# A new static order of instructions on every engine of a chunked linear-attention kernel

## The chip, the core and the metric

The kernel runs on one core of a Trainium2 chip. The metric is the device time of one execution in microseconds (us); lower is better. The time before is 1025.33 us, the median of 3 runs (1024.25 to 1025.99).

## What is computed

The reference takes x of shape (2, 4096, 512) and, per token, does this:

```
outer(h)  = LN(h + routed_attention(h)) * ln_g + ln_b
x1 = x  + 0.5 * outer(LN(x))
x2 = x1 + linear_attention(LN(x1))          # 16 heads of width 32, causal
y  = x2 + 0.5 * outer(LN(x2))

linear_attention(x):
  q, k, v = x @ Wq.T, x @ Wk.T, x @ Wv.T
  pq, pk  = elu(q) + 1, elu(k) + 1
  S_t = S_(t-1) + pk_t (outer) v_t ;  z_t = z_(t-1) + pk_t
  out_t = (pq_t S_t) / (pq_t . z_t + eps) ;  result = out @ Wo.T + bo
```

Both kernels leave out the routed attention inside the two outer blocks and compute LN(LN(h)) * ln_g + ln_b there; the linear attention is computed whole. The recurrence over t is done in chunks of 128 tokens.

## The kernel before, in words

**Tiles.** A chunk is 128 tokens of each of the two batch rows (b = 0, 1); there are 32 chunks. Matrices are split into a high and a low half in f16 and each product is made of three passes (`PASSES`), so one projection of one batch row is 12 matmuls of 128x512 (`project`, L1122). Per chunk and batch row TensorE does: `project_k`, `project_q`, `project_v` (from XT, the transposed normalised x), four groups of `scores` (KS times QS, into the two banks SC), two halves of `attend` (the chunk's own part and the carried state SS, into AV), two halves of `update` (the state's increment, also into AV), and `project_out` (from AT, the transposed attention output).

**Stages.** The body of one step handles several chunks. For a step whose `now` is chunk s, the scores and the attention belong to s, the projections of q, k, v to s+1, the loading and first normalisation (`front_*`) to s+2, the final normalisation and the store (`back_*`, `store_y`) to s-1. The step's `prev` is the same with all chunks one lower, so a body ends the previous chunk and starts the next. `run` unrolls the first five and the last six bodies and loops over the rest, two bodies a turn. As the end of one body is followed by the start of the next, an operation that is moved from `prev` at the top to `now` at the bottom has not moved at all; only the cyclic order matters.

**Engines.** Each engine has a block of its own with a list of operations and a hand-written order (`body`: SyncE L345, GpSimd L499, ScalarE L691, VectorE L1020, TensorE L1230). Nothing but semaphores ties the engines: an operation first waits for its producers and for the readers of the buffer that it overwrites, and everything behind it in its engine's order waits too. XT, QN, ATTN, AT and the two banks PJ have a single buffer per batch row.

**SyncE** issues every transfer, in this order per chunk: `next_x` (L286, load of 512 KB of x), `store_y` (L341, store of 512 KB), `turn_x(0)`, `turn_x(1)` (L296, DMA transposes XH to XT), `turn_k(1)`, then for the next chunk's tiles `turn_k(0)` (L309, KN to KS), `turn_q(0)` (L322, QN to QS), `turn_attn(0)` (L333, ATTN to AT), `turn_q(1)`, `turn_attn(1)`. `turn_x(b)` must wait until `project_v(b)` has read the old XT.

**TensorE**'s order per chunk: k(0), k(1), scores(1,0), scores(1,1), q(0), scores(1,2), scores(1,3), attend(0), q(1), update(0), v(0), attend(1), v(1), then scores(0,0) of the next chunk, update(1,0), update(1,1), scores(0,1), out(0), scores(0,2), scores(0,3), out(1). The first `project_k(0)` of the next chunk waits for `x_turned[0]`.

**The chain from the attention to the next x.** After `attend(1)`: `sums(1)` (ScalarE L671), `reciprocals(1)` (VectorE L938), `quotient(1)` (L949), `attn_half(1)` (ScalarE L679), `attn_low(1)` (VectorE L968), then SyncE: `turn_attn(1)`, `next_x`, `store_y`, `turn_x(0)`.

**Hand-offs of the bank PJ[0].** `project_k(0)` fills it, `exp_relu_k(0)` (ScalarE L602, L603) and `phi_k(0)` (VectorE L914) read it, then `project_q(0)` may start. `exp_relu_q(0)` (L611), `phi_q(0)` (L900), `q_half(0)` (L620) and `low_q(0)` (VectorE L907) follow, then `project_v(0)` may start. After it `low_v(0)`, then `project_out(0)`, read by `add_out(0)` (VectorE L979). `x1_bias` (GpSimd L415) needs `add_out(1)`, and `front_x1(0)` (VectorE L853) needs `x1_bias`.

Of the kernel before, what the change touches and what calls it, by code (L numbers as in the profile page):

```python
# [12 lines left out]
GROUPS = E // P  # L13
# [51 lines left out]
def build(nc, x, Wq, Wk, Wv, Wo, attn_bo, ln_g, ln_b, out):  # L65
    with ExitStack() as ctx:
# [196 lines left out]
        def _(sp):  # L263
# [80 lines left out]

            def body(st):  # L345
                now, prev = ops(st), ops(st.before())
                prev.turn_k(0)
                prev.turn_q(0)
                prev.turn_attn(0)
                prev.turn_q(1)  # L350
                prev.turn_attn(1)
                prev.next_x()
                prev.store_y()
                prev.turn_x(0)
                prev.turn_x(1)
                prev.turn_k(1)

            first = ops(Step(0, -2))
            first.next_x()
            first.turn_x(0)  # L360
            first.turn_x(1)
            run(sp, body)

            sp.wait_ge(y_stored.sem, y_stored.at(steps - 1))
# [3 lines left out]
        def _(pool):  # L368
# [129 lines left out]

            def body(st):  # L499
                now, prev = ops(st), ops(st.before())  # L500
                prev.spread_k(0)
                prev.cut(1, 3)
                prev.split_a(1, 0)
                prev.spread_q(0)
                prev.split_a(1, 1)
                prev.split_a(1, 2)
                prev.split_a(1, 3)
                prev.spread_q(1)
                prev.split_s(0)
                prev.rstd1_of_x1()  # L510
                now.rstd0_of_x()
                prev.spread_k(1)
                now.cut(0, 1)
                now.split_a(0, 0)
                now.split_a(0, 1)
                now.cut(0, 3)
                now.x1_bias()
                now.rstd2_of_x2()
                now.split_a(0, 2)
                now.split_a(0, 3)  # L520
                now.cut(1, 1)
                prev.split_s(1)

            first = ops(Step(0, -2))
            first.rstd0_of_x()
# [1 line left out]
            first.rstd1_of_x1()  # L527
            norms(1)
            run(pool, body)


        @block.scalar
        def _(act):
# [10 lines left out]
            def w_half(j):  # L544

                m = W_ORDER[j]
                act.wait_ge(scales_done, j // 2 + 1)
                for c in range(GROUPS):
                    k = j * GROUPS + c
                    act.wait_ge(wT_filled, k + 1)  # L550
                    a.activation(wT[m][:, HI, c], W_BANKS[k][:], ACT.Copy, scale=w_scale[:, m:m + 1]).then_inc(wT_hi, 1)
# [139 lines left out]
            def body(st):  # L691
                now, prev = ops(st), ops(st.before())
                opening, following = st.number and st.chunk(0) == -1, st.number and st.chunk(0) == 0
                prev.split_a(1, 0)
                prev.sums(0)
                prev.q_half(0)
                prev.split_a(1, 1)
                prev.split_a(1, 2)
                prev.split_a(1, 3)
                prev.exp_relu_q(1)  # L700
                if following:
                    w_half(3)
                prev.attn_half(0)
                prev.s_half(0)
                prev.q_half(1)
                prev.k_half(1)
                prev.sums(1)
                prev.v_half(0)
                prev.attn_half(1)
                prev.normalise(0)  # L710
                prev.normalise(1)
                prev.v_half(1)
                prev.x_half(0)
                prev.x_half(1)
                now.copy_scores(0, 1)
                now.front_scale(0)
                now.split_a(0, 0)
                now.split_a(0, 1)
                now.copy_scores(0, 3)
                now.split_a(0, 2)  # L720
                now.front_scale(1)
                prev.s_half(1)
                now.split_a(0, 3)
                now.exp_relu_k(0)
                now.back_scale(0)
                now.back_scale(1)
                now.k_half(0)
                now.exp_relu_k(1)
                if opening:
                    w_half(2)  # L730
                now.copy_scores(1, 1)
                now.exp_relu_q(0)
                now.copy_scores(1, 3)

            square(0)
# [11 lines left out]
            square(3)  # L747
            w_half(1)
            run(act, body)


        @block.vector
        def _(dve):
# [49 lines left out]
            def w_low(j):  # L803

                m = W_ORDER[j]
                for c in range(GROUPS):
                    k = j * GROUPS + c
                    dve.wait_ge(wT_hi, k + 1)
                    v.scalar_tensor_tensor(wT[m][:, LO, c], W_BANKS[k][:], w_scale[:, m:m + 1], wT[m][:, HI, c],
                                           ALU.mult, ALU.subtract).then_inc(wT_lo, 1)  # L810
# [209 lines left out]
            def body(st):  # L1020
                now, prev = ops(st), ops(st.before())
                opening, following = st.number and st.chunk(0) == -1, st.number and st.chunk(0) == 0
                prev.phi_q(0)
                now.front_stats(0)
                prev.reciprocals(0)
                prev.mask(1, 2)
                prev.front_mean1(0)
                prev.quotient(0)
                prev.low_q(0)
                prev.front_stats1(1)  # L1030
                now.front_mean(0)
                prev.add_s(0)
                prev.phi_q(1)
                if following:
                    w_low(3)
                prev.front_mean1(1)
                prev.attn_low(0)
                now.front_stats(1)
                prev.low_q(1)
                prev.back_y(1)  # L1040
                prev.reciprocals(1)
                prev.quotient(1)
                prev.low_v(0)
                prev.attn_low(1)
                prev.low_k(1)
                now.front_mean(1)
                now.mask(0, 0)
                prev.add_s(1)
                prev.x_low(0)
                prev.low_v(1)  # L1050
                prev.add_out(0)
                prev.x_low(1)
                prev.out_stats(0)
                now.mask(0, 2)
                prev.add_out(1)
                now.front_gain(0)
                prev.out_mean(0)
                now.front_gain(1)
                prev.out_stats(1)
                prev.out_mean(1)  # L1060
                now.front_x1(0)
                now.front_x1(1)
                now.phi_k(0)
                now.back_gain(0)
                now.back_gain(1)
                now.mask(1, 0)
                now.low_k(0)
                now.back_y(0)
                now.front_stats1(0)
                now.phi_k(1)  # L1070
                if opening:
                    w_low(2)

            first = ops(Step(0, -2))
            first.front_stats(0)
# [17 lines left out]
            w_low(1)  # L1093
            scales(1)
            run(dve, body)


        @block.tensor
        def _(pe):
# [130 lines left out]
            def body(st):  # L1230
                now, prev = ops(st), ops(st.before())
                opening, following = st.number and st.chunk(0) == -1, st.number and st.chunk(0) == 0
                prev.project_q(1)
                if following:
                    w_transposes(3 * GROUPS, 4 * GROUPS)
                prev.update(0, 0)
                prev.update(0, 1)
                prev.project_v(0)
                prev.attend(1, 0)
                prev.attend(1, 1)  # L1240
                prev.project_v(1)
                now.scores(0, 0)
                prev.update(1, 0)
                prev.update(1, 1)
                now.scores(0, 1)
                prev.project_out(0)
                now.scores(0, 2)
                now.scores(0, 3)
                prev.project_out(1)
                now.project_k(0)  # L1250
                now.project_k(1)
                if opening:
                    w_transposes(2 * GROUPS, 3 * GROUPS)
                now.scores(1, 0)
                now.scores(1, 1)
                now.project_q(0)
                now.scores(1, 2)
                now.scores(1, 3)
                now.attend(0, 0)
                now.attend(0, 1)  # L1260

            w_transposes(0, 2 * GROUPS)
            run(pe, body)


# [24 lines left out]
```

## Time and profile before

| what | value |
|---|---|
| median of 3 runs | 1025.33 us |
| the profiled execution, its own time | 1025.5 us |
| its span, first to last instruction | 1023.8 us |
| mean granted TensorE clock | 0.962 |
| PE busy | 909.5 us (89%) |
| DVE busy | 837.4 us (82%) |
| ACT busy | 757.8 us (74%) |
| POOL busy | 714.4 us (70%) |
| DMA, share of 16 engines | 66.1% |

The span is 1.7 us shorter than the execution's own time. The timeline says when an instruction began and how long it ran, with the idle time before it and its releaser in square brackets. The chain names, step by step, what released the next. "Landing" is the time from the issue of a transfer to its completion.

### The profile page before, as it was taken

To read this page: it belongs to the slowest core of one execution; us is meant where nothing else is said; L and a number is where in the kernel's file an instruction comes from. 1 tells how busy PE (TensorE), PEld (TensorE's weight loads), DVE (VectorE), ACT (ScalarE), POOL (GpSimd) and SP (SyncE) were. 2 spreads that over 40 slices of the span, in tenths; PEclk is the share of its full clock that TensorE was granted. 3 is DMA by queue.
4 is the path that set the end of the run, shared out by engine and by line. 5 is a ranking of instruction groups with operands and counts; after the bars stand their busy time and mean duration, and the time that the engine had idled before them with its cause. 6 is when DMAs were issued, how large, how long until landed. Compare 5 with 4: busy or idle time off the path is not lost.

```text
span 1023.8 us, 29832 instructions
## 1 busy us (share of the span) xinstructions
PE 909.5 (89%) x10240; PEld 524.7 (51%) x10240; DVE 837.4 (82%) x1513; ACT 757.8 (74%) x1327; POOL 714.4 (70%) x879
## 2 busy tenths in 40 slices
PE   1468999999999999999999999999999999999974
PEld 1234555555555555555555555555455555555542
DVE  3466988888888888988888889888888888878763
ACT  4367877788777777887777778877777788778761
POOL 1136877867787778777777787777677777767762
PEclk8678999999999999999999999999999999999996
DMA  7145678876666677666666777566577756667872
GB/s 256 21 71 100 133 135 163 166 143 120 141 143 139 138 164 164 145 126 133 139 140 137 163 164 144 123 137 139 126 150 164 161 131 119 137 131 126 142 125 62
DMA packets 421405, 139.81 MB, mean 137 GB/s; under 512 B 402544, under 2 KB 402544, under 8 KB 421360
## 3 DMA queue, kind: packets, MB, share of 16 engines
q1 hardware_dynamic: 421360, 139.24, 66.1%
q8 instruction: 25, 0.41, 0.2%
q14 instruction: 20, 0.16, 0.0%
HBM read 21.76 MB, written 16.78 MB: 38 GB/s over the span
## 4 chain that ended last, share of the span: by engine, by line
PE 57%; DMA 15%; SPq 8%; issue 6%; DVE 6%; ACT 4%; POOL 0%; ACTq 0%; DVEq 0%; POOLq 0%
PE PJ L1125 40%; DMA XT<-XH 14%; PE AV L1198 7%; SPq L333 3%; PE SC L1175 3%; PE AV L1210 3%; PE AV L1195 2%; DVE ATTN L968 2%; PE PJ L1224 2%; DVE TP L949 2%; ACT ATTN L679 1%; SPq L286 1%; SPq L341 1%; SPq L322 1%; ACT DEN L671 1%
## 5 line engine op out<-in xcount | busy, mean ns | idle before, releaser
L1125 PE MATMUL PJ<-wT,XT 128*128 128x512 f16 x2304 | 535.6, 385 | 61.2 <-DMA XT<-XH 51.6
L1125 PEld LDWEIGHTS PJ<-wT,XT 128*128 128x128 f16 x2304 | 217.1, 99 | 320.4 <-DMA XT<-XH 63.1
L472 POOL TENSOR_TENSOR A<-AM,A 128x512 f16<-128x512 f32 x256 | 291.1, 1157 | 12.2 <-ACT A L652 12.2
L652 ACT ACTIVATE A<-AM 128x512 f16<-128x512 f32 x256 | 151.3, 634 | 43.1 <-DVE AM L891 41.6
L1224 PE MATMUL PJ<-wT,AT 128*128 128x512 f16 x768 | 179.0, 383 | 1.6 <-DMA AT<-ATTN 1.6
L464 POOL TENSOR_SCALAR_AFFINE_SELECT AM<-AM 128x512 f32<-128x512 f32 x128 | 81.4, 636 | 105.0 <-ACT AM L642 102.6
L1224 PEld LDWEIGHTS PJ<-wT,AT 128*128 128x128 f16 x768 | 72.9, 99 | 80.2 <-issue 3.5
L1198 PE MATMUL AV<-VN,A 128*128 128x33 f16 x3072 | 112.8, 178 | 0.0
L1195 PE MATMUL AV<-SS,QS 128*128 128x33 f16 x1024 | 109.7, 178 | 3.2 <-POOL A L472 3.2
L1198 PEld LDWEIGHTS AV<-VN,A 128*128 128x128 f16 x3072 | 107.7, 96 | 3.7
L602 ACT ACTIVATE PHI<-PJ,inv_scale 128x512 f32<-128x512 f32 x64 | 43.6, 681 | 79.4 <-PE PJ L1125 79.4
L1195 PEld LDWEIGHTS AV<-SS,QS 128*128 128x128 f16 x1024 | 98.4, 96 | 7.1 <-POOL A L472 3.5
L415 POOL TENSOR_TENSOR X1BO<-X,obias 128x1024 f32<-128x1024 f32 x32 | 75.4, 2356 | 23.4 <-DVE X L979 22.2
L1175 PE MATMUL SC<-QS,KS 96*128 96x128 f16 x1024 | 83.9, 219 | 7.3 <-DVE AM L891 4.8
L891 DVE TENSOR_TENSOR AM<-SC,causal 128x512 f32<-128x512 f32 x128 | 86.2, 673 | 4.3 <-PE SC L1175 4.3
L1175 PEld LDWEIGHTS SC<-QS,KS 96*128 96x128 f16 x1024 | 68.5, 98 | 38.5 <-DVE AM L891 5.2
L979 DVE SCALAR_TENSOR_TENSOR X<-PJ,out_scale,X1BO 128x512 f32<-128x512 f32 x64 | 48.1, 751 | 39.7 <-PE PJ L1224 39.7
L642 ACT ACTIVATE AM<-SC 128x512 f32<-128x512 f32 x128 | 77.1, 602 | 3.7 <-PE SC L1175 3.7
L495 POOL TENSOR_TENSOR SS<-S,SC_HI 128x528 f16<-128x528 f32 x62 | 73.8, 1190 | 0.0
L620 ACT ACTIVATE QN<-PJ,f_scale 128x1024 f16<-128x1024 f32 x64 | 72.5, 1133 | 0.9 <-DVE PJ L900 0.8
L914 DVE SCALAR_TENSOR_TENSOR PHI<-PHI,PJ 128x512 f32<-128x512 f32 x64 | 43.5, 679 | 34.4 <-ACT PJ L603 34.4
L480 POOL COPY KN<-KN 128x1024 f16<-128x1024 f16 x64 | 66.8, 1043 | 3.0 <-ACT KN L630 3.0
(98 smaller groups left out, 1529.7 us busy)
## 6 DMA issues: line engine op xcount, KB each, us to landing
X<-in_L_attn_x_dram SPq DMA_DIRECT2D x32, 512.0 KB, 4.2
out_dram<-Y SPq DMA_DIRECT2D x32, 512.0 KB, 4.9
A<-in_L_attn_Wk_dram SPq DMA_DIRECT2D x1, 1024.0 KB, 7.8
A<-in_L_attn_Wq_dram SPq DMA_DIRECT2D x1, 1024.0 KB, 10.1
QS<-in_L_attn_Wv_dram SPq DMA_DIRECT2D x1, 1024.0 KB, 12.2
QS<-in_L_attn_Wo_dram SPq DMA_DIRECT2D x1, 1024.0 KB, 14.4
XT<-XH SPq DMA_TRANSPOSE x64, 4.4
KS<-KN SPq DMA_TRANSPOSE x64, 4.3
```

Source lines behind the costliest of these rows:

```text
L415: g.tensor_tensor(X1BO[:, st.parity(1)], X1[:], obias[:].unsqueeze(1).to_broadcast([P, BATCH, E]), ALU.add).then_inc(x1bo_done.sem, 1)
L464: g.affine_select(out=am, in_=am, compare_op=ALU.is_ge, fill=0.0, base=0, pattern=[[0, QUADS], [1, C]], channel_multiplier=-1).then_inc(sc ...
L472: g.tensor_tensor(A[:, b, LO, hg], AM[:, k % 4], A[:, b, HI, hg], ALU.subtract).then_inc(a_lo.sem, 1)
L495: g.tensor_tensor(SS[:, b], S[:, b], SC_HI[:, b], ALU.subtract).then_inc(s_lo.sem, 1)
L642: a.activation(AM[:, k % 4], SC[hg % 2][:], ACT.Copy, scale=SUM_DOWN).then_inc(sc_copied.sem, 1)
L652: a.activation(A[:, b, HI, hg], AM[:, k % 4], ACT.Copy).then_inc(a_hi.sem, 1)
L891: v.tensor_tensor(AM[:, k % 4].rearrange("p (h q) -> p h q", h=QUADS), SC[hg % 2][:].rearrange("p (h q) -> p h q", h=QUADS), causal[:].uns ...
L1125: ins = t_.matmul(PJ[b], XT[:, w, c, b * C:(b + 1) * C], wT[m_][:, m, c, :], start=(c, w, m) == todo[0], stop=(c, w, m) == todo[-1])
L1175: ins = t_.matmul(SC[hg % 2][:, h * C:(h + 1) * C], KS[cur][0:STACK, head, b * C:(b + 1) * C], QS[cur][0:STACK, head, b * C:(b + 1) * C], ...
L1195: t_.matmul(to, QS[cur][:, head, b * C:(b + 1) * C], SS[:, b, hf, j * DA:(j + 1) * DA], start=True, stop=False)
L1198: ins = t_.matmul(to, A[:, b, w, hg, h * C:(h + 1) * C], VN[cur][:, b, m, head, :], start=False, stop=(w, m) == PASSES[-1])
L1224: ins = t_.matmul(PJ[b], AT[:, b, w, c * C:(c + 1) * C], wT[3][:, m, c, :], start=(c, w, m) == todo[0], stop=(c, w, m) == todo[-1])
```

## The change

No operation is added, removed or altered; the lists of operations in the five `body` functions are put in another order, and a few lines move from `prev` at the top of a body to `now` at its end without moving in the cycle. In the cyclic order:

- SyncE: `store_y` goes from between `next_x` and `turn_x(0)` to between `turn_q(0)` and `turn_attn(0)`; `turn_q(1)` goes from between the two `turn_attn` to behind `turn_k(1)`. `next_x` stays right ahead of `turn_x(0)`.
- TensorE: `project_q(0)` goes ahead of scores(1,0) and (1,1), `attend(0)` ahead of scores(1,2) and (1,3); the next chunk's scores(0,1) goes ahead of `update(1,0)`, and `update(1,1)` behind scores(0,3).
- ScalarE, VectorE, GpSimd: many operations move by a few places, as the diff shows.

The diff, with one line of context, the common indentation cut:

```diff
@@ -346,9 +346,7 @@
 now, prev = ops(st), ops(st.before())
-prev.turn_k(0)
 prev.turn_q(0)
+prev.store_y()
 prev.turn_attn(0)
-prev.turn_q(1)
 prev.turn_attn(1)
 prev.next_x()
-prev.store_y()
 prev.turn_x(0)
@@ -356,2 +354,4 @@
 prev.turn_k(1)
+prev.turn_q(1)
+now.turn_k(0)
 
@@ -500,5 +500,4 @@
 now, prev = ops(st), ops(st.before())
-prev.spread_k(0)
-prev.cut(1, 3)
 prev.split_a(1, 0)
+prev.cut(1, 3)
 prev.spread_q(0)
@@ -507,8 +506,8 @@
 prev.split_a(1, 3)
-prev.spread_q(1)
-prev.split_s(0)
 prev.rstd1_of_x1()
-now.rstd0_of_x()
-prev.spread_k(1)
+prev.split_s(0)
+prev.spread_q(1)
 now.cut(0, 1)
+prev.spread_k(1)
+now.rstd0_of_x()
 now.split_a(0, 0)
@@ -517,2 +516,3 @@
 now.x1_bias()
+prev.split_s(1)
 now.rstd2_of_x2()
@@ -521,3 +521,3 @@
 now.cut(1, 1)
-prev.split_s(1)
+now.spread_k(0)
 
@@ -693,4 +693,2 @@
 opening, following = st.number and st.chunk(0) == -1, st.number and st.chunk(0) == 0
-prev.split_a(1, 0)
-prev.sums(0)
 prev.q_half(0)
@@ -705,24 +703,23 @@
 prev.q_half(1)
-prev.k_half(1)
-prev.sums(1)
 prev.v_half(0)
+prev.sums(1)
 prev.attn_half(1)
+prev.k_half(1)
 prev.normalise(0)
+prev.x_half(0)
+now.copy_scores(0, 1)
 prev.normalise(1)
 prev.v_half(1)
-prev.x_half(0)
 prev.x_half(1)
-now.copy_scores(0, 1)
-now.front_scale(0)
 now.split_a(0, 0)
-now.split_a(0, 1)
 now.copy_scores(0, 3)
-now.split_a(0, 2)
+now.split_a(0, 1)
+now.front_scale(0)
 now.front_scale(1)
 prev.s_half(1)
-now.split_a(0, 3)
 now.exp_relu_k(0)
-now.back_scale(0)
-now.back_scale(1)
+now.split_a(0, 2)
+now.split_a(0, 3)
 now.k_half(0)
+now.back_scale(0)
 now.exp_relu_k(1)
@@ -730,4 +727,7 @@
     w_half(2)
+now.back_scale(1)
 now.copy_scores(1, 1)
 now.exp_relu_q(0)
+now.split_a(1, 0)
+now.sums(0)
 now.copy_scores(1, 3)
@@ -1022,12 +1022,7 @@
 opening, following = st.number and st.chunk(0) == -1, st.number and st.chunk(0) == 0
-prev.phi_q(0)
-now.front_stats(0)
-prev.reciprocals(0)
-prev.mask(1, 2)
-prev.front_mean1(0)
-prev.quotient(0)
 prev.low_q(0)
-prev.front_stats1(1)
-now.front_mean(0)
+prev.back_gain(1)
 prev.add_s(0)
+prev.front_mean1(1)
+prev.back_y(1)
 prev.phi_q(1)
@@ -1035,7 +1030,5 @@
     w_low(3)
-prev.front_mean1(1)
+now.front_stats(0)
 prev.attn_low(0)
-now.front_stats(1)
 prev.low_q(1)
-prev.back_y(1)
 prev.reciprocals(1)
@@ -1044,27 +1037,29 @@
 prev.attn_low(1)
-prev.low_k(1)
-now.front_mean(1)
 now.mask(0, 0)
-prev.add_s(1)
+prev.low_k(1)
 prev.x_low(0)
+now.front_stats(1)
+now.front_mean(0)
+now.front_mean(1)
 prev.low_v(1)
-prev.add_out(0)
 prev.x_low(1)
-prev.out_stats(0)
+prev.add_s(1)
+prev.add_out(0)
 now.mask(0, 2)
+prev.out_stats(0)
 prev.add_out(1)
 now.front_gain(0)
-prev.out_mean(0)
 now.front_gain(1)
 prev.out_stats(1)
+prev.out_mean(0)
 prev.out_mean(1)
 now.front_x1(0)
-now.front_x1(1)
 now.phi_k(0)
+now.front_x1(1)
+now.front_stats1(0)
 now.back_gain(0)
-now.back_gain(1)
-now.mask(1, 0)
+now.front_mean1(0)
+now.front_stats1(1)
 now.low_k(0)
-now.back_y(0)
-now.front_stats1(0)
+now.mask(1, 0)
 now.phi_k(1)
@@ -1072,2 +1067,7 @@
     w_low(2)
+now.back_y(0)
+now.phi_q(0)
+now.reciprocals(0)
+now.quotient(0)
+now.mask(1, 2)
 
@@ -1232,5 +1232,2 @@
 opening, following = st.number and st.chunk(0) == -1, st.number and st.chunk(0) == 0
-prev.project_q(1)
-if following:
-    w_transposes(3 * GROUPS, 4 * GROUPS)
 prev.update(0, 0)
@@ -1242,5 +1239,4 @@
 now.scores(0, 0)
-prev.update(1, 0)
-prev.update(1, 1)
 now.scores(0, 1)
+prev.update(1, 0)
 prev.project_out(0)
@@ -1248,2 +1244,3 @@
 now.scores(0, 3)
+prev.update(1, 1)
 prev.project_out(1)
@@ -1253,9 +1250,12 @@
     w_transposes(2 * GROUPS, 3 * GROUPS)
+now.project_q(0)
 now.scores(1, 0)
 now.scores(1, 1)
-now.project_q(0)
-now.scores(1, 2)
-now.scores(1, 3)
 now.attend(0, 0)
 now.attend(0, 1)
+now.scores(1, 2)
+now.scores(1, 3)
+now.project_q(1)
+if opening:
+    w_transposes(3 * GROUPS, 4 * GROUPS)
 
```

## Rows read from the trace of the kernel before

**Rows 1.** The page, part 4: shares of the chain that ended last, by line

```profile
PE PJ L1125 40%; DMA XT<-XH 14%; PE AV L1198 7%; SPq L333 3%; PE SC L1175 3%; PE AV L1210 3%; PE AV L1195 2%; DVE ATTN L968 2%; PE PJ L1224 2%; DVE TP L949 2%; ACT ATTN L679 1%; SPq L286 1%; SPq L341 1%; SPq L322 1%; ACT DEN L671 1%
```

**Rows 2.** Waits: engine line waited for, us in total, times, longest

```profile
PE PJ L1125 <- DMA XT<-XH: 51.6, 29, 2.9
```

**Rows 3.** The chain, 511 to 522 us: start us, us, what

```profile
511.14 0.28 ACT DEN L671
...
513.10 0.70 DVE ATTN L968
...
513.88 1.23 SPq L333
...
515.54 0.39 SPq L286
...
516.32 0.39 SPq L341
...
516.97 4.92 DMA XT<-XH
```

**Rows 4.** Timeline of PE, 490 to 540: start us, us, engine line, xcount, [idle before]

```profile
493.01 5.35 PE L1125 MATMUL PJ<-wT,XT 128*128 128x512 f16 x24 [1.91 <-DMA XT<-XH]
...
514.80 2.75 PE L1224 MATMUL PJ<-wT,AT 128*128 128x512 f16 x12
...
517.84 2.76 PE L1224 MATMUL PJ<-wT,AT 128*128 128x512 f16 x12
521.94 5.35 PE L1125 MATMUL PJ<-wT,XT 128*128 128x512 f16 x24 [1.35 <-DMA XT<-XH]
527.13 0.61 PE L1175 MATMUL SC<-QS,KS 96*128 96x128 f16 x8
527.58 2.75 PE L1125 MATMUL PJ<-wT,XT 128*128 128x512 f16 x12
...
535.70 2.75 PE L1125 MATMUL PJ<-wT,XT 128*128 128x512 f16 x12
```

**Rows 5.** Timeline of SP: the loads of chunk 4 and of chunk 31

```profile
106.30 0.51 SPq L286 DMA_DIRECT2D X<-in_L_attn_x_dram  x1
...
897.54 0.51 SPq L286 DMA_DIRECT2D X<-in_L_attn_x_dram  x1
```

**Rows 6.** Line L296, window 107:109: turn_x(0), a load before it, no store

```profile
L296 SPq DMA_TRANSPOSE XT<-XH x1: 1244/1244/1244, 107.6 to 107.6; - x1
...
DMA to landing us min/median/max: 3.8/3.8/3.8
```

**Rows 7.** Line L296, window 930:932: turn_x(0), a store 1.42 before it, no load

```profile
L296 SPq DMA_TRANSPOSE XT<-XH x1: 1696/1696/1696, 930.3 to 930.3; - x1
...
DMA to landing us min/median/max: 4.0/4.0/4.0
```

**Rows 8.** Timeline of SP, 510 to 540: q(1), k(1) with the next k(0), attn(0)

```profile
510.65 2.10 SPq L322 DMA_TRANSPOSE QS<-QN  x1
...
521.35 12.49 SPq L309 DMA_TRANSPOSE KS<-KN  x2
...
538.04 1.24 SPq L333 DMA_TRANSPOSE AT<-ATTN  x1
```

**Rows 9.** Line L333 (turn_attn), window 200:900, 48 of them: landing

```profile
DMA to landing us min/median/max: 3.0/3.0/5.0
```

**Rows 10.** Line L309 (turn_k), window 200:900, 48 of them: landing

```profile
DMA to landing us min/median/max: 4.2/4.3/6.0
```

**Rows 11.** Timeline of DVE, 510 to 540: add_out(1), phi_k(0), low_q(0), attn_low(0)

```profile
520.63 0.75 DVE L979 SCALAR_TENSOR_TENSOR X<-PJ,out_scale,X1BO 128x512 f32<-128x512 f32 x1 [0.50 <-PE PJ L1224]
...
526.01 0.69 DVE L914 SCALAR_TENSOR_TENSOR PHI<-PHI,PJ 128x512 f32<-128x512 f32 x1 [0.62 <-ACT PJ L603]
...
534.43 0.74 DVE L907 SCALAR_TENSOR_TENSOR QN<-PJ,f_scale,QN 128x512 f16<-128x512 f32 x1
...
537.29 0.66 DVE L968 SCALAR_TENSOR_TENSOR ATTN<-TP,ATTN 128x512 f16<-128x512 f32 x1
```

**Rows 12.** Timeline of POOL, 510 to 540: two splits of A, x1_bias

```profile
517.88 2.27 POOL L472 TENSOR_TENSOR A<-AM,A 128x512 f16<-128x512 f32 x2 [0.40 <-ACT A L652]
...
521.54 2.36 POOL L415 TENSOR_TENSOR X1BO<-X,obias 128x1024 f32<-128x1024 f32 x1 [0.80 <-DVE X L979]
```

More of the change, by code:

```diff
@@ L500, in body @@
                 now, prev = ops(st), ops(st.before())
-                prev.spread_k(0)
+                prev.split_a(1, 0)
                 prev.cut(1, 3)
-                prev.split_a(1, 0)
                 prev.spread_q(0)
@@ L507, in body @@
                 prev.split_a(1, 3)
+                prev.rstd1_of_x1()
+                prev.split_s(0)
                 prev.spread_q(1)
-                prev.split_s(0)
-                prev.rstd1_of_x1()
+                now.cut(0, 1)
+                prev.spread_k(1)
                 now.rstd0_of_x()
-                prev.spread_k(1)
-                now.cut(0, 1)
                 now.split_a(0, 0)
@@ L693, in body @@
                 opening, following = st.number and st.chunk(0) == -1, st.number and st.chunk(0) == 0
-                prev.split_a(1, 0)
-                prev.sums(0)
                 prev.q_half(0)
@@ L705, in body @@
                 prev.q_half(1)
+                prev.v_half(0)
+                prev.sums(1)
+                prev.attn_half(1)
                 prev.k_half(1)
-                prev.sums(1)
-                prev.v_half(0)
-                prev.attn_half(1)
                 prev.normalise(0)
+                prev.x_half(0)
+                now.copy_scores(0, 1)
                 prev.normalise(1)
                 prev.v_half(1)
-                prev.x_half(0)
                 prev.x_half(1)
-                now.copy_scores(0, 1)
+                now.split_a(0, 0)
+                now.copy_scores(0, 3)
+                now.split_a(0, 1)
                 now.front_scale(0)
-                now.split_a(0, 0)
-                now.split_a(0, 1)
-                now.copy_scores(0, 3)
-                now.split_a(0, 2)
                 now.front_scale(1)
                 prev.s_half(1)
+                now.exp_relu_k(0)
+                now.split_a(0, 2)
                 now.split_a(0, 3)
-                now.exp_relu_k(0)
+                now.k_half(0)
                 now.back_scale(0)
-                now.back_scale(1)
-                now.k_half(0)
                 now.exp_relu_k(1)
@@ L1044, in body @@
                 prev.attn_low(1)
+                now.mask(0, 0)
                 prev.low_k(1)
+                prev.x_low(0)
+                now.front_stats(1)
+                now.front_mean(0)
                 now.front_mean(1)
-                now.mask(0, 0)
+                prev.low_v(1)
+                prev.x_low(1)
                 prev.add_s(1)
-                prev.x_low(0)
-                prev.low_v(1)
                 prev.add_out(0)
-                prev.x_low(1)
+                now.mask(0, 2)
                 prev.out_stats(0)
-                now.mask(0, 2)
                 prev.add_out(1)
                 now.front_gain(0)
-                prev.out_mean(0)
                 now.front_gain(1)
                 prev.out_stats(1)
+                prev.out_mean(0)
                 prev.out_mean(1)
                 now.front_x1(0)
+                now.phi_k(0)
                 now.front_x1(1)
-                now.phi_k(0)
+                now.front_stats1(0)
                 now.back_gain(0)
-                now.back_gain(1)
+                now.front_mean1(0)
+                now.front_stats1(1)
+                now.low_k(0)
                 now.mask(1, 0)
-                now.low_k(0)
-                now.back_y(0)
-                now.front_stats1(0)
                 now.phi_k(1)
@@ L1242, in body @@
                 now.scores(0, 0)
+                now.scores(0, 1)
                 prev.update(1, 0)
-                prev.update(1, 1)
-                now.scores(0, 1)
                 prev.project_out(0)
@@ L1253, in body @@
                     w_transposes(2 * GROUPS, 3 * GROUPS)
+                now.project_q(0)
                 now.scores(1, 0)
                 now.scores(1, 1)
-                now.project_q(0)
+                now.attend(0, 0)
+                now.attend(0, 1)
                 now.scores(1, 2)
                 now.scores(1, 3)
-                now.attend(0, 0)
-                now.attend(0, 1)
+                now.project_q(1)
+                if opening:
+                    w_transposes(3 * GROUPS, 4 * GROUPS)
             w_transposes(0, 2 * GROUPS)
```

## The prediction

> **What bounds the kernel now.** I read four views in this order. The chain that ended last comes first: the projections carry 40% of it, and the next largest entry is no work but a transfer, the turning of x, at 14% [rows 1]. The list of waits says what TensorE pays for that: 51.6 us in 29 waits, 1.78 us a chunk [rows 2]. The timeline of TensorE shows that this is all it pays in the steady part: project_k(0) begins at 493.01 and again at 521.94, with 1.35 us idle right before the second and none between [rows 4]. So a chunk took 28.93 us, of which 27.58 is TensorE's own pace. Over the 27 chunks between the loads at 106.30 and 897.54 a chunk takes 29.30 us on average [rows 5], which less the mean wait of 1.78 is again 27.5. Last, the chain over one such wait shows what makes x late [rows 3]: sums(1) at 511.14, attn_low(1) at 513.10, turn_attn(1) issued at 513.88, the load at 515.54, the store at 516.32, turn_x(0) at 516.97, landed 4.92 later. Everything between 511.14 and 516.97 is 5.83 us of small steps, and the two copies stand in line ahead of the transfer for which TensorE waits.
>
> The sum is made against the profiled execution, 1025.5 us (span 1023.8 and 1.7 around it), which is 0.2 above the median of 1025.33. About 0.2% (2 us) is what a measurement of this kernel can tell from no change.
>
> **The change, part by part.** No instruction is added or removed, so each part is a question of what stands ahead of what.
>
> *The store leaves the line ahead of turn_x(0).* Its issue slot is worth 516.97 - 516.32 = 0.65 us [rows 3]. Its data no longer go first either. The landing was 4.92 us behind a load and a store [rows 3]. Where only a load stood ahead, issued 1.29 us before (106.30 against 107.59), it was 3.8 us [rows 5, 6]; where only a store did, 1.42 us before, 4.0 us [rows 7]. In the new order the load is issued only some 0.65 us ahead of x, so I add the missing 0.64 to 3.8 and take 4.4. Bounds: 3.0, the usual landing of turn_attn, a transfer of the same size with nothing just ahead [rows 9], and 4.92, no gain at all. I take 4.4 because the run with a load ahead is the nearest to the new case.
>
> The Trainium skill bears on this ("DMA: Bandwidth & Descriptors", "Queues, rings and completion order" and "Anatomy of one DMA"): transfers of one issuer are taken up in the order of their ring on each DMA engine, and its fit for a DMA is 2.0 us plus bytes over 436 GB/s. By its rate the store's 512 KB would hold x up by 1.2 us, an estimate from that page, and with the issue slot the saving would be 1.85 a chunk, more than the whole mean wait, and the time 974. The rows give less, 0.5, so the sum goes by them.
>
> *The loop after it.* From project_k(0) to sums(1) is 511.14 - 493.01 = 18.13 us [rows 3, 4]. TensorE's new order has the same operations in that stretch, only q(0) and attend(0) are earlier within it, so it stays 18.13. Then 5.83 - 0.65 = 5.18 to the issue of turn_x(0), 4.4 to its landing, 0.05 to the start of TensorE: 27.76 us. That stands against TensorE's own 27.58. So x is late by about 0.2 instead of 1.35. The mean chunk was 0.37 above the one that I read (29.30 against 28.93), mostly from later landings; I leave a part of it in and take 27.9. **Saved: 29.3 - 27.9 = 1.4 us, 29 times: 41 us.**
>
> *turn_q(1) goes behind turn_k(1).* It was issued at 510.65, far ahead of its use [rows 8]; now it is the fourth transpose in line. Turn_x(0) is issued at 23.3 of the chunk, and turn_k(1) followed it by 4.38 (521.35 against 516.97) [rows 3, 8]. One more slot of 2.1 [rows 8] puts q(1) at 29.8, which is 2.0 after the next project_k(0). With 4.3, the middle landing of the equal-sized turn_k [rows 10], it is there at 6.3; TensorE wants it for scores(1,0) after k(0), k(1) and q(0), that is 5.19 + 2.6 = 7.8 [rows 4]. Cost nothing, with 1.5 of cover; with the longest landing, 6.0 [rows 10], 0.2 a chunk. This is also why q(0) had to go ahead of these scores: at the old place they would start at 5.2 and wait 1.1.
>
> *q(0) ahead of the scores.* It used to begin 5.64 after k(0) (527.58 - 521.94), with the scores as cover from 5.19 on [rows 4]. Phi_k(0), which frees the bank, began at 526.01 and took 0.69, so it ended at 4.76 [rows 11]. The cover shrinks from 0.88 to 0.43: nothing, while VectorE is in time. VectorE's list puts phi_k(0) behind one front_x1 instead of two, which helps. If phi_k(0) is late, all of it is paid.
>
> *low_q(0) ahead of v(0).* It ended at 535.17, 13.23 after k(0), and v(0) began at 13.76 [rows 4, 11]. In the new ScalarE list copy_scores(1,3) goes ahead of q_half(0) and q(0) itself is ready 0.45 earlier; the two about cancel. Nothing, with 0.5 of cover.
>
> *store_y ahead of turn_attn(0).* SyncE waits there for back_y(1), but VectorE does back_y(1) before attn_low(0) in the new list, so this adds no wait of its own for the turn_attn(0) queued behind. What costs is VectorE: back_gain(1) and back_y(1), 0.7 each, now stand ahead of attn_low(0). It began at 15.35 and was turned at 16.10 [rows 8, 11]; I expect it turned at 17.3 to 17.5. Landing in 3.0 it is there at 20.5; project_out(0) wants it at 514.80 - 493.01 = 21.79, less what x no longer delays, 21.4 [rows 4, 9]. Nothing, with 0.9 of cover. With a store 1.5 us ahead and the longest landing seen, 5.0 [rows 9], it is 1.0 late.
>
> *GpSimd.* split_s(1), spread_k(1) and rstd0 change places around the splits of A. The work is the same; what must not slip is x1_bias, which began at 521.54, right behind add_out(1) (520.63 + 0.75), for front_x1(0) waits for it and phi_k(0) now stands directly behind that [rows 11, 12]. I cost it at nothing; see the rivals.
>
> *The ends.* The first four chunks and the drain are latencies between engines in which TensorE idles anyway; nothing below nor above 3 us.
>
> **Sum:** 1025.5 - 41 = 984.5, and for the median 984.
>
> **Rivals.** *B. The landing does not move.* The change is called "x ahead of the load and the store", but in the diff the load still stands right ahead of turn_x(0). If it is the load that holds x up, only the issue slot is saved: 0.65 x 28 = 18 us, 1007. For: the load's data are the nearer. Against: rows 6 and 7, both 0.9 to 1.1 below 4.92. *C. turn_attn(0) lands late* by up to 1.0 and eats most of the gain: 0.4 x 29 = 12, 1013. For: it lies behind the store now. Against: in the old order even turn_x(0) with two copies ahead lost only 1.9 against 3.0. *D. Slower: x1_bias is late on GpSimd.* In the new list rstd0 stands ahead of the two splits of A, the cut and x1_bias, and it waits for front_mean(1) on VectorE, which comes behind x_low(0). If this pushes x1_bias behind the two splits, 2.27 us [rows 12], phi_k(0) is late by 2.27 less its cover of 0.43: TensorE waits 1.84 at q(0) in every chunk. 27.76 + 1.84 = 29.6, 0.3 above now, 29 times: 1034. It decides once x1_bias starts more than about 2.0 us after add_out(1) ended (0.16 now, 0.43 of cover, 1.4 of gain). Against: it had 0.80 idle before it [rows 12]. *E. No wait at all is left:* 1025.5 - 51.6 = 974.
>
> **How the numbers follow.** Forecast with E as its lower end, 0.63; B 0.12; C 0.08; D 0.12; a mixture of small late hand-offs that leaves no change, 0.05. The likeliest case runs from 974 to 997. The range reaches from 974 over B to 1009. Faster 0.83, same 0.05, slower 0.12.
>
> **What would show it.** The wait of PE L1125 for XT falls from 51.6 us to under 12; turn_x(0) is issued some 0.65 after the load and lands in 4.2 to 4.6; loads follow each other every 27.8 to 28.0 us; PE shows no new idle before q(0) (a wait for DVE L914), before v(0) (for DVE L907) or before L1224 (for AT). I am wrong if the landing stays near 5 (B), if L1224 waits for AT (C), or if q(0) waits for PHI with POOL L415 behind it (D).

## The result and the profile after

The changed kernel takes 978.43 us (median of 4 runs, 977.9 to 979.8) against 1025.66 (4 runs) for the kernel before in the same session; the ratio is 0.9542, with a 95% interval of 0.9525 to 0.9558. The forecast was 984, with a range of 974 to 1009. The span of the profiled run fell from 1023.8 to 976.8 us, by 47.0.

The page of the changed kernel: span, busy time, and the chain by line, which answers to [rows 1].

```profile
span 976.8 us, 29868 instructions
PE 903.1 (92%) x10240; PEld 524.9 (54%) x10240; DVE 837.8 (86%) x1513; ACT 757.5 (78%) x1327; POOL 713.5 (73%) x879
...
PE PJ L1125 46%; PE PJ L1224 13%; PE AV L1198 7%; PE SC L1175 5%; PE AV L1210 4%; DMA XT<-XH 4%; DMA AT<-ATTN 3%; PE AV L1195 2%; DVE AM L891 1%; SPq L322 0%; DVE PJ L900 0%; DVE ATTN L968 0%; DVE XH L879 0%; POOL A L472 0%; ACT A L652 0%
```

TensorE's busy time fell by 6.4 us (909.5 to 903.1) and that of the other engines changed by less than 1, so some 41 of the 47 us are idle time of TensorE that has gone. The clock does not explain the gain: from 200 to 850 us the granted TensorE clock is 1.00, its upper level, in both kernels. The turning of x fell from 14% of the chain to 4%. The waits of the changed kernel over the whole run, which answer to [rows 2]:

```profile
PEld PJ L1125 <- DMA XT<-XH: 17.3, 25, 4.0
...
PE PJ L1125 <- DMA XT<-XH: 10.3, 5, 3.8
...
PE PJ L1224 <- DMA AT<-ATTN: 4.3, 7, 1.2
```

PEld is TensorE's loading of its stationary operand. The matmuls' wait for XT is 10.3 us for 51.6, and nearly all of it lies at the start: in the first 200 us it is 9.6 (9.5 before), in the stretch from 200 to 850 us it is 0.7 (38.1 before), and no other wait of the matmuls there is above 0.3. The transfer queue in the same place as [rows 3], the timeline of SP of the changed kernel:

```profile
511.24 1.32 SPq L309 DMA_TRANSPOSE KS<-KN  x1
513.73 2.00 SPq L322 DMA_TRANSPOSE QS<-QN  x1
516.10 0.57 SPq L341 DMA_DIRECT2D out_dram<-Y  x1
517.69 4.79 SPq L333 DMA_TRANSPOSE AT<-ATTN  x2
522.85 0.39 SPq L286 DMA_DIRECT2D X<-in_L_attn_x_dram  x1
523.57 3.35 SPq L296 DMA_TRANSPOSE XT<-XH  x2
527.26 1.79 SPq L309 DMA_TRANSPOSE KS<-KN  x1
529.38 2.11 SPq L322 DMA_TRANSPOSE QS<-QN  x1
```

The landing of that turn_x(0) (line L296, window 523 to 524.5), and TensorE's timeline beside it, as in [rows 4]:

```profile
L296 SPq DMA_TRANSPOSE XT<-XH x1: 1237/1237/1237, 523.6 to 523.6; - x1
DMA to landing us min/median/max: 4.5/4.5/4.5
```

```profile
500.32 7.94 PE L1125 MATMUL PJ<-wT,XT 128*128 128x512 f16 x36
...
514.02 2.75 PE L1125 MATMUL PJ<-wT,XT 128*128 128x512 f16 x12
...
521.86 2.75 PE L1224 MATMUL PJ<-wT,AT 128*128 128x512 f16 x12
...
525.31 2.75 PE L1224 MATMUL PJ<-wT,AT 128*128 128x512 f16 x12
528.07 7.94 PE L1125 MATMUL PJ<-wT,XT 128*128 128x512 f16 x36
```

The store is gone from between the load and x. Turn_x(0) is issued at 523.57 and lands 4.45 us later, at 528.02, just as project_out(1) ends (525.31 + 2.75): there is no idle mark on the row at 528.07 any more, where there was 1.35 us. Between the two project_k(0) lie 27.75 us for 28.93. The landing of this one chunk is typical: over the chunks from 200 to 850 us the median landing of turn_x(0) is 4.3 us (4.0 to 5.6), for 5.2 (4.7 to 5.6) in the kernel before.

### The profile page after: what moved, and what is told of

It is laid out like the page before. It is cut to its first block, busy times and chain, and to the rows that moved or that the text cites. A ratio compares the mean times of both kernels' runs of the same rounds, so it can differ in the third digit from the quotient of the medians.

```text
span 976.8 us, 29868 instructions
## 1 busy us (share of the span) xinstructions
PE 903.1 (92%) x10240; PEld 524.9 (54%) x10240; DVE 837.8 (86%) x1513; ACT 757.5 (78%) x1327; POOL 713.5 (73%) x879
## 4 chain that ended last, share of the span: by engine, by line
PE 78%; DMA 6%; DVE 4%; issue 3%; SPq 1%; ACT 1%; POOL 1%; DVEq 0%; POOLq 0%; ACTq 0%
PE PJ L1125 46%; PE PJ L1224 13%; PE AV L1198 7%; PE SC L1175 5%; PE AV L1210 4%; DMA XT<-XH 4%; DMA AT<-ATTN 3%; PE AV L1195 2%; DVE AM L891 1%; SPq L322 0%; DVE PJ L900 0%; DVE ATTN L968 0%; DVE XH L879 0%; POOL A L472 0%; ACT A L652 0%
## 5 line engine op out<-in xcount | busy, mean ns | idle before, releaser
L1125 PE MATMUL PJ<-wT,XT 128*128 128x512 f16 x2304 | 524.4, 382 | 18.9 <-DMA XT<-XH 10.3
L1224 PEld LDWEIGHTS PJ<-wT,AT 128*128 128x128 f16 x768 | 70.6, 98 | 82.9 <-DMA AT<-ATTN 5.5
L1175 PE MATMUL SC<-QS,KS 96*128 96x128 f16 x1024 | 78.6, 220 | 2.4 <-issue 1.9
L1175 PEld LDWEIGHTS SC<-QS,KS 96*128 96x128 f16 x1024 | 65.9, 98 | 25.3 <-issue 2.3
L679 ACT ACTIVATE ATTN<-TP 128x512 f16<-128x512 f32 x64 | 39.3, 614 | 33.7 <-DVE TP L949 33.7
L1210 PEld LDWEIGHTS AV<-VN,KN 128*128 128x128 f16 x1984 | 61.2, 96 | 7.3
```

Of the source, the lines that this page charges most:

```text
L1125: ins = t_.matmul(PJ[b], XT[:, w, c, b * C:(b + 1) * C], wT[m_][:, m, c, :], start=(c, w, m) == todo[0], stop=(c, w, m) == todo[-1])
L1175: ins = t_.matmul(SC[hg % 2][:, h * C:(h + 1) * C], KS[cur][0:STACK, head, b * C:(b + 1) * C], QS[cur][0:STACK, head, b * C:(b + 1) * C], ...
L1210: ins = t_.matmul(AV2[:, hf, j * DA:(j + 1) * DA], stack, VN[cur][:, b, m, head, :], start=m == HI, stop=m == LO)
L1224: ins = t_.matmul(PJ[b], AT[:, b, w, c * C:(c + 1) * C], wT[3][:, m, c, :], start=(c, w, m) == todo[0], stop=(c, w, m) == todo[-1])
```

## The experiments

All ratios are to the kernel before on the same chip, with a 95% interval. "A chunk" is the distance between the load of chunk 4 and that of chunk 31, over 27, as in [rows 5]; it was 29.30 us before and is 27.84 in the changed kernel, whose two loads are these:

```profile
102.78 0.52 SPq L286 DMA_DIRECT2D X<-in_L_attn_x_dram  x1
...
854.38 0.51 SPq L286 DMA_DIRECT2D X<-in_L_attn_x_dram  x1
```

**1. The store alone is moved, in the kernel before.**

```diff
                 prev.next_x()
-                prev.store_y()
                 prev.turn_x(0)
                 prev.turn_x(1)
                 prev.turn_k(1)
+                prev.store_y()
```

> The kernel before with one edit: the store is issued behind turn_k(1) instead of between the load and turn_x(0). All other orders are the old ones. Theory S (the store ahead of turn_x is the cause, issue slot and data both): turn_x(0) is issued 0.65 us earlier and lands in about 4.4 instead of 4.9 to 5.6; the wait of the k projection for XT falls from 51.6 us to under 15, loads are some 28.0 us apart, the median is 980 to 992. Rival O (the new order as a whole is needed, because the old one runs into other waits once x is early): the XT wait falls, but scores(1,0) at its old place waits for KS, whose turn_k(1) is issued 20.7 us into the chunk and is wanted 5.2 after the next start; with landings of 4.3 to 6.0 that is up to 1 us a chunk, and the median is 1000 to 1015.

Measured: 976.09 us, 0.9542 (0.9514 to 0.9570), a little below the 980 to 992 expected; a chunk is 27.67. This one line does all that the change does. The waits over the whole run:

```profile
PEld PJ L1125 <- DMA XT<-XH: 18.2, 29, 3.1
...
PE PJ L1125 <- DMA XT<-XH: 9.0, 11, 2.9
```

The median landing of turn_x(0) from 200 to 850 us is 3.9 us (3.7 to 4.4). Rival O falls: the scores wait for KS once in the whole run, for 0.6 us.

**2. The store is put back, in the changed kernel.**

```diff
-                prev.store_y()
                 prev.turn_attn(0)
                 prev.turn_attn(1)
                 prev.next_x()
+                prev.store_y()
                 prev.turn_x(0)
```

> The changed kernel with one edit: the store is put back between the load and turn_x(0). Theory S: the wait for XT is back, 1.2 to 1.8 us a chunk, the median is 1015 to 1027. Rival L (the load, not the store, delays the landing, so that only the issue slot of 0.65 counts): 0.65 x 28 = 18 over the changed kernel, 996. Rival O (the gain is in the orders of the compute engines): 978 to 985.

Measured: 1022.63 us, 0.9988 (0.9967 to 1.001), as expected: the whole gain is gone. The wait and the landing of the turn_x(0) issued at 519.18:

```profile
PE PJ L1125 <- DMA XT<-XH: 50.5, 29, 4.0
```

```profile
L296 SPq DMA_TRANSPOSE XT<-XH x1: 1949/1949/1949, 519.2 to 519.2; - x1
DMA to landing us min/median/max: 5.5/5.5/5.5
```

So in the changed kernel the gain hangs on the place of the store, and by run 1 moving the store is enough. It is not the only way to the gain: see run 8.

**3. Slot or data?** The kernel before, in its old order, stores only 16 rows of each chunk (32 KB for 512 KB) and leaves out the rest of y.

```diff
-sp.dma_start(out[:, bass.ds(back * C, C), :].rearrange("b p e -> p b e"), Y[:])
+sp.dma_start(out[0, bass.ds(back * C, 16), :], Y[0:16, 0])
```

> The kernel before, every order as it was, but the store moves only 16 rows of one batch row (32 KB for 512 KB); the rest of y is left out of the output. The issue slot stays, the data all but go. Theory S with both parts: turn_x(0) is issued as late as before but lands in about 3.8 to 4.3 instead of 4.9 to 5.6, 0.8 to 1.2 us a chunk, so the median is 992 to 1003. Rival L: the landing stays at 4.9 to 5.6 and the median at 1020 to 1026.

Measured: 983.08 us, 0.9606 (0.9581 to 0.9631), a chunk 27.99. The issue slot is still there, 0.62 us of it:

```profile
525.64 0.41 SPq L286 DMA_DIRECT2D X<-in_L_attn_x_dram  x1
526.32 0.36 SPq L341 DMA_DIRECT2D out_dram<-Y  x1
526.94 3.37 SPq L296 DMA_TRANSPOSE XT<-XH  x2
```

```profile
L296 SPq DMA_TRANSPOSE XT<-XH x1: 1247/1247/1247, 526.9 to 526.9; - x1
DMA to landing us min/median/max: 3.9/3.9/3.9
```

The data are the larger part: without them a chunk is 1.31 us shorter (29.30 - 27.99), and the median landing of turn_x(0) is 4.0 us for 5.2. Taking the slot away as well (run 1) brings only 0.32 more; that TensorE's own pace ends the gain there is an inference. The time is below what either theory had said, 992 at best. The run takes the store's data away from every transfer, not only from x, so it does not by itself tell what they cost x from what they cost the others; but x was the transfer for which TensorE waited.

**4. x right ahead of the load too, in the changed kernel,** as the change's description has it.

```diff
-                prev.next_x()
                 prev.turn_x(0)
                 prev.turn_x(1)
+                prev.next_x()
                 prev.turn_k(1)
```

> The changed kernel with the load moved behind turn_x(1), so that x is really turned ahead of the load and the store. If what is left of the wait for XT (10.3 us, all in five places) is start-up, and TensorE is now the bound at some 27.5 us a chunk, nothing comes of it: 975 to 980. If late landings still cost a part of each chunk: 970 to 974, with turn_x(0) landing in 3.1 to 3.3. If q(1), pushed back by one more slot, now comes late for scores(1,0): 980 to 990 and a wait for QS.

Measured: 983.16 us, 0.9606 (0.9580 to 0.9632), a chunk 27.96. x lands in 3.1 us (the median of 46), and still this kernel is some 5 us slower than the changed one (0.9606 against 0.9556 in run 9, on another chip), as the third of the expected cases has it: the load now stands ahead of k(1) and q(1). From 200 to 850 us the scores wait for QS in 14 places, 3.9 us in all, and in none in the changed kernel. One of the places, on TensorE:

```profile
538.08 0.62 PE L1175 MATMUL SC<-QS,KS 96*128 96x128 f16 x8 [0.26 <-DMA QS<-QN]
```

**5. The new order of SyncE alone, in the kernel before.** The edit is the SyncE part of the diff, its first two hunks; all other lists are old.

> The kernel before with the new order on SyncE alone (store ahead of turn_attn(0), turn_q(1) behind turn_k(1)); the compute engines keep the old orders. Theory (x is freed, and the rest of the new order only makes room for the later q(1) and store): the XT wait is gone, but two new waits come: scores(1,0) at its old place 5.2 us into the chunk waits for QS, which lands at 5.7 to 6.3, 0.5 to 1.1 us; and turn_attn(0) stands behind a store that waits for back_y(1), done only 18.2 us into the chunk in the old VectorE order, so that it lands at 21.5 to 22.5 for a project_out(0) at 21.4, 0.1 to 1.0 us. Together 990 to 1010. Rival (only the transfers matter, the rest is free): 975 to 982.

Measured: 1081.43 us, 1.0533 (1.0484 to 1.0582): slower, where I had expected 990 to 1010. The waits of matmuls, and one chunk of TensorE:

```profile
PE SC L1175 <- DMA QS<-QN: 44.8, 24, 2.3
...
PE PJ L1224 <- DMA AT<-ATTN: 32.6, 31, 3.1
```

```profile
509.76 2.76 PE L1224 MATMUL PJ<-wT,AT 128*128 128x512 f16 x12 [0.83 <-DMA AT<-ATTN]
...
515.40 5.34 PE L1125 MATMUL PJ<-wT,XT 128*128 128x512 f16 x24
522.55 0.62 PE L1175 MATMUL SC<-QS,KS 96*128 96x128 f16 x8 [1.81 <-DMA QS<-QN]
```

Both waits that I named came, and XT is no longer waited for in the steady part. Their sizes were 1.81 and 0.83 here, where I had 0.5 to 1.1 and up to 1.0, and what I had missed is that the late turn_attn(0) also makes q(1) late. The chain that ended last shows it, step by step:

```profile
504.36 0.75 DVE Y L1015
...
506.11 3.60 DMA AT<-ATTN
...
509.76 2.78 PE PJ L1224 x12
...
513.23 0.69 DVE XH L879
...
514.00 1.24 SPq L296
...
517.96 4.37 DMA QS<-QN
```

The store waits for back_y(1) (504.36), and turn_attn(0) waits behind it, so project_out(0) starts late. In VectorE's old list add_out(0), which needs project_out(0), stands ahead of x_low(1) (513.23), so turn_x(1) goes only at 514.00, 3.5 us behind turn_x(0), and k(1) and q(1) stand behind it in the queue. Q(1) is issued at 517.96, 2.56 us into the chunk, and lands 4.37 later, where the scores want it at 5.3. The new list of VectorE puts back_y(1) earlier and x_low(1) ahead of add_out(0): these moves are the room that the new order of the queue needs. No run tested them one by one.

**6. TensorE's old order alone, in the changed kernel.** The edit takes back the TensorE part of the diff, all of it.

> The changed kernel with TensorE's old order (scores(1,0) and (1,1) ahead of q(0), and so on); all else new. Theory: scores(1,0) then waits for q(1), issued 29.4 minus 28.07 = 1.3 us into the chunk and landing in 4.4, at 5.7, where it is wanted at 5.2: a wait for QS of about 0.5 us a chunk, median 988 to 996. Rival (TensorE's order is indifferent): 976 to 982.

Measured: 1013.77 us, 0.9879 (0.9831 to 0.9927), a chunk 28.91; 988 to 996 were expected. The wait is the one expected, its size is not:

```profile
521.30 0.62 PE L1175 MATMUL SC<-QS,KS 96*128 96x128 f16 x8 [0.86 <-DMA QS<-QN]
```

It is 0.86 us here and not 0.5, and 21.1 us in 23 places from 200 to 850 us, 0.92 each; a chunk is 1.07 longer than in the changed kernel. Run 1 has the whole gain with TensorE's old order, so q(0) ahead of the scores is no gain of its own; it pays for having moved turn_q(1).

**7 and 8. Which copy? Both behind turn_k(1), and the load alone behind turn_k(1),** in the kernel before, with all else old. Run 7 and run 8:

```diff
                 prev.turn_attn(1)
-                prev.next_x()
-                prev.store_y()
                 prev.turn_x(0)
                 prev.turn_x(1)
                 prev.turn_k(1)
+                prev.next_x()
+                prev.store_y()
```

```diff
                 prev.turn_attn(1)
-                prev.next_x()
                 prev.store_y()
                 prev.turn_x(0)
                 prev.turn_x(1)
                 prev.turn_k(1)
+                prev.next_x()
```

> The kernel before with the load and the store both issued behind turn_k(1), so that nothing but turn_attn(1) stands ahead of x; all else old. turn_x(0) should land in 3.0 to 3.3 as with nothing ahead. If the late landings that are left with the store moved (XT wait 9.0 us, 11 times, 27.67 us a chunk) still cost something: 27.4 to 27.5 us a chunk and 969 to 974. If TensorE is the whole bound there: 974 to 978, no better than with the store moved alone. If k(1) or the next K and Q transposes are pushed into a wait, 980 or more.

> The kernel before with the load issued behind turn_k(1) and the store left right ahead of turn_x(0): the mirror image of the run in which the store was moved. If it is the number of copies ahead that counts, whichever they are, x lands in about 4.0 and the median is 975 to 985. If the store is special (it writes to HBM) the landing stays near 5 and the median is 1000 to 1010.

Measured: both moved 976.91 us, 0.9510 (0.9466 to 0.9554), a chunk 27.68; the load alone 973.36, 0.9469 (0.9424 to 0.9515), a chunk 27.54. With only the store ahead, x lands in a median of 3.2 us, where 4.0 had been expected, nearly as fast as the 3.0 with nothing ahead. Run 8, SP's timeline and the landing:

```profile
547.94 0.39 SPq L341 DMA_DIRECT2D out_dram<-Y  x1
549.09 3.75 SPq L296 DMA_TRANSPOSE XT<-XH  x2
```

```profile
L296 SPq DMA_TRANSPOSE XT<-XH x1: 1301/1301/1301, 549.1 to 549.1; - x1
DMA to landing us min/median/max: 3.1/3.1/3.1
```

So either copy may be the one that goes, and removing the second brings nothing more. Why run 7 is not the faster one the traces show in part. From 200 to 850 us its VectorE waits for the store, now issued last, to have read Y, which has a single buffer; in run 8 there is no such wait:

```profile
DVE Y L1015 <- DMA out_dram<-Y: 8.2, 18, 0.8
```

In the same stretch TensorE waits for VectorE's PHI in 7 places, 2.0 us in all, and in run 8 in none. That the one leads to the other was not tested.

**9 to 12. Ranking on one chip, five rounds.** The changed kernel, runs 1 and 8 again, and the changed kernel with the load behind turn_q(1):

```diff
-                prev.next_x()
                 prev.turn_x(0)
                 prev.turn_x(1)
                 prev.turn_k(1)
                 prev.turn_q(1)
+                prev.next_x()
                 now.turn_k(0)
```

> The changed kernel once more, beside the three below on the same chip, to rank them: ratio to before 0.951 to 0.957 as in its first run.

> The kernel before with the store alone behind turn_k(1), once more. If moving one line does all that the new order does, its interval overlaps that of the changed kernel; if the whole order brings anything beyond, it is slower by more than 0.3%.

> The kernel before with the load alone behind turn_k(1), once more. Its one run had 27.54 us a chunk against 27.84 of the changed kernel, and 973.4 us: if that is real, it is 4 to 7 us below the changed kernel here too; if it was the chip, they are within 2 us.

> The changed kernel with the load behind turn_q(1), so that x, k(1) and q(1) all go ahead of it. x should land in 3.1 and q(1) be no later than in the changed kernel, so the wait for QS seen with the load right behind x (3.9 us, and 27.96 us a chunk) is gone: 27.5 to 27.7 us a chunk and 971 to 976. If it stays at 27.8 or more, what is left in the changed kernel is TensorE's own pace in its new order, and not transfers.

| kernel | us | ratio (95%) | a chunk, us |
|---|---|---|---|
| changed kernel | 979.54 | 0.9556 (0.9528 to 0.9585) | 27.85 |
| before, store behind k(1) | 978.37 | 0.9541 (0.9512 to 0.9571) | 27.83 |
| before, load behind k(1) | 971.56 | 0.9469 (0.9440 to 0.9499) | 27.50 |
| changed, load behind q(1) | 972.46 | 0.9495 (0.9467 to 0.9523) | 27.66 |

The kernel before with the load behind turn_k(1), one line moved, beats the changed kernel by 8.0 us: its interval lies wholly below, and that of run 8 lay below that of the changed kernel's first measurement too (0.9515 against 0.9525, in different sessions). Between it and the changed kernel with the load behind q(1) the intervals overlap. What the changed kernel still loses does not show as a wait of the matmuls but of the weight loads, for XT is the stationary operand, the one that is loaded. From 200 to 850 us, first the changed kernel, then the one with the load behind q(1), where no wait for XT is left:

```profile
PEld PJ L1125 <- DMA XT<-XH: 8.7, 21, 1.2
PEld PJ L1224 <- DMA AT<-ATTN: 0.4, 1, 0.4
```

```profile
PEld PJ L1224 <- DMA AT<-ATTN: 0.8, 2, 0.6
```

In the changed kernel x lands at the very end of project_out(1), so the first part of it can't be loaded for project_k(0) under the matmuls before it: 8.7 us over 21 chunks, 0.4 each. The two runs with the old orders differ in the same way: 11.4 us of this wait with the store behind k(1), 0.9 with the load behind k(1), and 6.8 us between their times. That this wait is the whole of the difference, 7 us in both pairs, is an inference and was not tested by itself.

## Why the prediction was right, and where it was off

**Place and mechanism: right.** The store ahead of turn_x(0) was named as the cause, and runs 1 and 2 show that its move is enough and that the gain of the changed kernel goes when it is put back. The loop closes as worked out: turn_x(0) is issued 23.25 us into the chunk that begins at 500.32 (523.57 - 500.32; 23.31 in the sum), and the next project_k(0) begins at 27.75 (27.76 in the sum). Rival B (the landing does not move) falls by medians of 4.3 us for 5.2, though its thought, that the load holds x up, is borne out by run 8: moving the load instead gains as much and more. C (turn_attn(0) late) is there only at the ends, 4.3 us in 7 places, for 1.6 before; D needed x1_bias 2.0 us after add_out(1): add_out(1) began at 528.10 for 0.75 and x1_bias at 528.93.

```profile
528.93 2.36 POOL L415 TENSOR_TENSOR X1BO<-X,obias 128x1024 f32<-128x1024 f32 x1 [0.33 <-DVE X L979]
```

E (no wait left) is nearest by the time, 974 for 978.4, and by the matmuls' waits, 1.0 us in all in the steady part. But x is still a little late: the weight loads wait 0.4 us for it in 21 chunks of that stretch, and the kernels without this wait have chunks of 27.50 and 27.66 us. That is the main case of the prediction, x late by about 0.2. Nor could all 51.6 us have gone: 9.5 of them lie in the first 200 us and are 9.6 in the changed kernel.

**The store's data were mis-sized.** The prediction took the landing from 4.92 to 4.4, 0.5 us, beside 0.65 for the slot. The 4.4 was met: the median is 4.3. The 4.92 was the wrong end: it was one chunk, and a low one, as the median before is 5.2, so the landing fell by 0.9. Run 3, where slot and load stay as they are, puts the data at 1.2 us of landing and 1.31 us a chunk. The row with only a store ahead [rows 7] was no good guide either: its 4.0 is from the drain at the end, and in the steady part of run 8 it is 3.2.

The Trainium skill's rate ("DMA: Bandwidth & Descriptors", "Anatomy of one DMA") had given 1.2 for the 512 KB. The page states this fit for DMAs issued from GpSimd, and these are issued from SyncE; run 3 agrees with it all the same, better than the rows that I weighed against it. The saving of 1.85 a chunk that the estimate from this page gave was not reached: it was 1.47.

That the sum was close has two reasons. One is judgement: I took TensorE's own pace, 27.58 in the chunk that I read, as the floor of a chunk, whatever the landing gives, and no run has a chunk below 27.50. The other is luck: of the 0.37 us by which the mean chunk exceeded the one read I left 0.14 in, and the 0.23 that I so counted as saved made up for more than half of the 0.4 by which the landing's 0.5 fell short.

**A chunk: 27.9 predicted, 27.84 measured.** The saving is 29.305 - 27.837 = 1.47 us, over 27 chunks 39.6 us, where 1.4 had been foreseen, 37.8.

**The ends were costed at nothing, within 3 us.** The load of chunk 4 is issued at 102.78 for 106.30, 3.5 us earlier. From the load of chunk 31 to the end it is 976.8 - 854.38 = 122.4 for 1023.8 - 897.54 = 126.3, 3.8 us less, of which two of the 29 waits of the sum cover 2.8. In all 3.5 + 39.6 + 3.8 = 47 us, where the sum had 41 (29 x 1.4): of the miss of 6, 1.8 are from the chunks, 3.5 from the start and 1.0 from the drain. So the start is the term that was put at nothing and was not. What made it shorter is open: it is not the store, for run 2, with the store put back, has this load at 103.65, and run 1, with the store alone moved, at 105.51. Run 9, the changed kernel again, has it at 103.56. A part may be the clock: the granted clock of the first 66 us was 0.77 in the changed kernel's profile for 0.72 before, and 0.74 in run 9.

**The covers.** All held, though closely. VectorE in the chunk that begins at 500.32:

```profile
504.54 0.68 DVE L914 SCALAR_TENSOR_TENSOR PHI<-PHI,PJ 128x512 f32<-128x512 f32 x1
...
512.81 0.74 DVE L907 SCALAR_TENSOR_TENSOR QN<-PJ,f_scale,QN 128x512 f16<-128x512 f32 x1
```

Phi_k(0) ends at 4.90 (4.76 before, wanted at 5.19), so 0.29 is left of the 0.43; low_q(0) ends at 13.23, as before, for a v(0) at 13.70; turn_attn(0) goes out at 517.69, 17.37, where 17.3 to 17.5 was said. Q(1) is issued 1.3 us into the next chunk instead of 2.0, and no wait for QS shows. The prediction said that at their old place the scores would wait 1.1 for it; run 6 has 0.92 on average.

## What to carry to other kernels

When one engine waits for a transfer, look at what stands right ahead of it in the same queue, and count the bytes ahead as well as the issue slot; a copy that nobody needs soon belongs behind the urgent one. But look at what it then stands ahead of: in the changed kernel the load right ahead of k(1) and q(1) cost some 5 us against leaving it where it was, and behind them it gained 7. A reordering of five engines can be one useful line and a set of moves that pay for each other: taken alone, the new order of the queue made the old kernel 5% slower, so try the single line before the package.

## What was not expected of the hardware

- The two copies ahead do not simply add up. From 200 to 850 us turn_x(0) lands in a median of 3.0 us with neither ahead (run 7), 3.2 with the store 1.1 us ahead (run 8), 3.9 with the load 1.0 ahead (run 1), 4.3 with the load 0.7 ahead (changed kernel), and 5.2 with both (kernel before, the load 1.3 to 1.4 and the store 0.65 ahead). The distances differ too, and no run separates them from the kind of copy.
- Two full copies ahead also lengthen the issue of the transpose itself. The two kernels' line L296, from 200 to 850 us, first before, then changed:

```profile
L296 SPq DMA_TRANSPOSE XT<-XH x44: 1599/1979/2387, 225.7 to 842.6; - x44
```

```profile
L296 SPq DMA_TRANSPOSE XT<-XH x46: 1232/1237/1745, 219.0 to 829.7; - x46
```

  That is 0.74 us less per transpose (the medians). One full copy ahead does not do it: the median for turn_x(0) is 1.25 us in run 1 and 1.30 in run 8; nor does the load with the 32 KB store, 1.26 in run 3. Everything queued behind x goes out earlier too: the pair's row is 3.35 us for 4.05. This is how q(1) came to be 0.7 earlier than reckoned.
